# A graph network's third node stage: norm scale and shift moved into a copy, two bias matmuls removed, walk words loaded inside a batch

## Chip, core and metric

The kernel runs on one core of one Trainium2 chip. The metric is device time in microseconds (us), the median of several runs. The engines are PE (TensorE, matmuls; PEld is its loading of weights, PEldq or PEq its sequencer, which decodes instructions), DVE (VectorE), ACT (ScalarE), POOL (GpSimd) and SP (SyncE, here only a queue that issues DMAs). Each engine runs its own instructions in order; between engines there are only semaphores.

## The reference

Four graph layers over 50000 nodes of 128 floats, on 25000 edges, each followed by `x = layernorm(x + layer(x))`. The change touches how the third layer (GATv2, 4 heads) and the sums over neighbours of the layers before it are computed:

```
def _gatv2(x, ...):
    xl = (x @ Wl.T + bl).reshape(n, H, D)
    ...
    alpha = ex / (den[dst] + 1e-16)
    agg = segment_sum(xl[src] * alpha[:, :, None], dst, n)
    return agg.mean(axis=1) + conv_bias
h  = _gatv2(x, ...)
x1 = _layernorm(x + h, g1, beta1)             # (r - mean) * rstd * g1 + beta1
f  = gelu(x1 @ W1.T + b1) @ W2.T + b2
x  = _layernorm(x + _layernorm(x1 + f, g2, beta2))
```

The weights alpha of a node's edges sum to 1 in each head, so the mean over the heads of the bias bl comes out of a node's sum unchanged. All data is float32; a float32 matmul is two passes of the array in the trace, a bfloat16 one is one pass.

## The kernel before

The program is a chain of stages with a barrier after each. Three places matter.

**Walks** (`walk`, stages e0, e1a, e1b, before the second layer's node stage). POOL gathers the rows of the edges' sources (L998, 196 DMAs for each walk, four to a group). DVE makes one-hot matrices (L1013). PE adds six steps to a batch, 66 batches in a walk, 12 matmul instructions (24 passes, L1056) in each: `add_steps` first loads the batch's eight table words into registers with two loads of four (L1045), waits for the one-hots (L1049), the gathered rows (L1050) and begun tiles (L1051), and issues the matmuls, whose operands are addressed by these words. The body is a loop of three batches. ACT takes finished tiles out of PSUM.

**Edge sum** (`edge_sum` with `PrepareGatv2`, stage at 2123 to 2416 us). 196 chunks of 128 edges, in 28 groups of seven. For a chunk PE multiplies the source rows by Wl into one of seven PSUM banks (L1235, 512 columns) and adds the bias by a bfloat16 matmul with three rows (L1236). ACT scales the first head (L1221). DVE adds the other three (L1251), two chunks interleaved, and adds to each chunk the running sum of the chunk before it (L707); after a pair of chunks it waits for its last result and gives the banks back (L1264). After a group it waits again and signals (L713), and POOL scatters the group's seven chunks to DRAM by indirect DMAs (L684), only at rows where a node's edges end.

**Third node stage** (`node_gatv2`, names n_..., 2426 to 3207 us). 98 blocks of 512 rows, on a software pipeline: in every step of a loop of six each engine does its parts for blocks of different age, in an order written out at the end of its function (`pipeline(pe, (2, turn1), (7, product3), (6, turn3), (3, ffn2), (2, ffn1))`: the number is the age). For a block:
- DVE adds x and the edges' sum (L2247), takes statistics (L2254, L2263); POOL makes the reciprocal deviation and the shift (L1339 to L1345); ACT normalises (L1354).
- PE turns the rows over (L2329), ACT copies them out of PSUM (`move1`, L2373), PE multiplies by W1 (`ffn1`, L2336), ACT applies gelu (L2379).
- PE sums in one PSUM bank (`ffn2`): the biases by a bfloat16 matmul with three rows (L2301), x1 by a matmul with a diagonal of g1 (L2304), the product with W2 (L2307).
- DVE takes the second statistics from that bank (L2254, n_stats<-n_y_ps), POOL the deviation (L1332, L1334), DVE normalises (L2271), multiplies by g2 (L2277), adds the residual (L2282), takes third statistics; ACT normalises again (L1354, n_x3s), PE turns (L2315), ACT copies (L2361), PE multiplies by the next layer's weights (L2322), ACT keeps the result (L2367, L2368).

DVE's order in a step is: first add, second norm (four blocks back), first statistics, times g2, first aggregation, residual, second statistics (three back), third statistics, second aggregation, third aggregation. POOL's is: second deviation, third, first, then the addition of beta2. Before the loop DVE folds g1 into W1 and into the identity, and splits beta1 + b2 into three bfloat16 rows (L2233 to L2240); ACT spreads these by DMA.

## Time and profile before

| | us |
|---|---|
| median of 3 runs | 4979.55 (4978.65 to 4981.04) |
| the profiled execution | 4979.08 |
| its span in the trace | 4977.4 |
| busy PE / DVE / ACT / POOL | 3368.8 / 3292.8 / 2328.2 / 3358.2 |
| first, second, third walk, PE's first to last matmul | 137.7 to 382.9, 737.3 to 987.9, 998.1 to 1250.3 |
| edge sum, DVE's first to last chunk | 2128.4 to 2400.2 |
| third node stage | 2426 to 3207 |

Since stages end in barriers, the time is the sum of the stages, and each is read by itself: which engine waits for nothing there, or which closed chain of waits repeats. What the profile calls the chain that ended last covers only the final stage.

### The profile page before, as it was taken

What the parts mean: (1) busy time and instruction counts of PE and PEld (TensorE: products, weight loads), DVE (VectorE), ACT (ScalarE), POOL (GpSimd) and SP (SyncE); (2) the same over time, 40 slices, a digit from 0 to 9 for tenths busy, and PEclk for the clock granted to TensorE, in tenths of its full rate; (3) what the DMA queues carried; (4) which work ended last, traced back from release to release, by engine and by line L of the source; (5) the groups of instructions that cost most, each with busy time, mean ns of one, the idle gap of its engine ahead of it and who ended that gap; (6) DMA issues with size and microseconds to landing.
All of it is one profiled execution on the core that took longest, in us unless ns stands there. A gap on an engine that the chain in (4) does not pass through costs nothing. (4 is left out here: it accounts for less than half of the span.)

```text
span 4977.4 us, 95692 instructions
## 1 busy us (share of the span) xinstructions
PE 3368.8 (68%) x21145; PEld 2475.2 (50%) x21146; DVE 3292.8 (66%) x13393; ACT 2328.2 (47%) x6751; POOL 3358.2 (67%) x4041
## 2 busy tenths in 40 slices
PE   0778867777885999699599999730004999321666
PEld 0676757677563444322266666520003777221566
DVE  6987874454785777778588888650804888623676
ACT  0556767667674444333288888500002444000566
POOL 3746757677455777357588888676674555673998
PEclk9999989999998999899799999855557999655888
DMA  4447869888897412001144444352115988341676
GB/s 95 147 141 231 256 194 266 243 254 258 260 287 247 133 52 53 26 30 38 61 143 137 145 137 145 109 154 46 33 41 193 293 294 275 110 117 52 190 224 196
DMA packets 592362, 784.61 MB, mean 158 GB/s; under 512 B 138226, under 2 KB 362150, under 8 KB 591610
## 3 DMA queue, kind: packets, MB, share of 16 engines
q1 hardware_dynamic: 430496, 532.37, 35.0%
q0 software_dynamic: 62848, 112.43, 9.3%
q10 hardware_dynamic: 98846, 138.05, 7.6%
q14 instruction: 129, 1.06, 0.1%
q8 instruction: 43, 0.70, 0.1%
HBM read 470.23 MB, written 317.95 MB: 158 GB/s over the span
## 5 line engine op out<-in xcount | busy, mean ns | idle before, releaser
L2889 POOL TENSOR_SCALAR n_hot<-node_of,d_krel 128x256 f32<-128x256 f32 x396 | 381.1, 976 | 65.3 <-ACTq L2945 65.3
L1354 ACT ACTIVATE n_r<-n_r,n_shift,n_rstd 128x128 f32<-128x128 f32 x784 | 321.6, 480 | 67.7 <-POOL n_shift L1345 62.7
L2917 PE MATMUL n_bank<-h_rows,n_hot 128*128 x1584 | 241.8, 322 | 144.3 <-POOL n_hot L2889 144.1
L2917 PEld LDWEIGHTS n_bank<-h_rows,n_hot 128*128 128x128 f32 x1584 | 229.4, 232 | 157.4 <-issue 157.4
L684 POOL DMA_INDIRECT agg<-e_msg,e_put_i x196 | 194.8, 994 | 164.3 <-DVEq L713 113.0
L1354 ACT ACTIVATE n_o<-n_y_ps,n_shift,n_rstd 128x128 f32<-128x128 f32 x784 | 292.7, 454 | 13.5 <-POOL n_shift L1625 13.3
L968 POOL DMA_INDIRECT by_src<-by_src_pay,by_src_place_i x196 | 207.7, 1060 | 120.5 <-DVE n_o L1532 64.3
L998 POOL DMA_INDIRECT x_rows<-x,d_other_i x196 | 191.0, 974 | 119.2 <-POOLq L102 59.7
L615 POOL DMA_INDIRECT agg_dst<-e_rows,e_put_i x196 | 195.2, 996 | 102.2 <-issue 59.4
L2510 POOL TENSOR_TENSOR n_u<-n_u 128x512 f32<-128x512 f32 x98 | 124.6, 1271 | 205.7 <-DVE n_u L2457 205.7
L2639 POOL DMA_INDIRECT h_rows<-h,d_other_i x196 | 202.5, 1033 | 76.2 <-issue 59.4
L998 POOL DMA_INDIRECT y_rows<-y,s_other_i x196 | 186.2, 950 | 90.7 <-issue 53.4
L1341 POOL TENSOR_TENSOR n_rstd<-n_rstd,minus_half 128x4 f32<-128x4 f32 x196 | 235.2, 1200 | 15.4
L2011 POOL DMA_INDIRECT e_rows<-h,e_other_i x196 | 194.4, 992 | 73.8 <-issue 59.4
L1913 DVE TENSOR_TENSOR lg_z<-lg_z_ps,lg_z 128x512 f32<-128x512 f32 x196 | 135.3, 690 | 162.5 <-ACT lg_z L1879 162.5
L1056 PE MATMUL e1b_bank<-y_rows,e1b_hot 128*128 x1584 | 199.6, 285 | 60.4 <-ACT e1b_bank L1181 33.0
L2307 PE MATMUL n_y_ps<-n_w,n_gt 128*128 128x128 f32 x1568 | 240.5, 276 | 0.0
L1056 PE MATMUL e1a_bank<-y_rows,e1a_hot 128*128 x1584 | 198.7, 284 | 58.9 <-ACT e1a_bank L1167 30.1
L1834 POOL DMA_INDIRECT lg_rows<-x,e_other_i x196 | 186.0, 949 | 77.8 <-issue 59.4
L998 POOL DMA_INDIRECT y_rows<-m,s_other_i x196 | 186.1, 949 | 74.7 <-issue 57.3
L1235 PE MATMUL e_xl_ps<-gat_wl,e_xg 128*128 128x512 f32 x392 | 223.4, 652 | 18.0 <-ACT e_xg L1208 18.0
L1056 PE MATMUL e_bank<-x_rows,e_hot 128*128 x1584 | 197.1, 282 | 51.1 <-ACT e_bank L1139 42.2
(516 smaller groups left out, 11424.8 us busy)
## 6 DMA issues: line engine op xcount, KB each, us to landing
n_ag<-agg_dst SPq DMA_DIRECT2D x196, 264.0 KB
n_hs<-h SPq DMA_DIRECT2D x196, 264.0 KB
n_xs<-x SPq DMA_DIRECT2D x196, 256.0 KB, 4.3
agg_dst<-e_ev SPq DMA_DIRECT2D x196, 132.0 KB
y<-n_o ACTq DMA_DIRECT2D x98, 264.0 KB, 3.5
e1a_fed<-y SPq DMA_DIRECT2D x196, 132.0 KB
m<-e1a_ev SPq DMA_DIRECT2D x196, 132.0 KB
e1b_fed<-m SPq DMA_DIRECT2D x196, 132.0 KB
```

Of the source, the lines that this page charges most:

```text
L615: pool.indirect_dma_start(out=agg, out_offset=bass.IndirectOffsetOnAxis(ap=e.put_i[:, c:c + 1], axis=0), in_=rows[:, c, :], in_offset=None ...
L684: pool.indirect_dma_start(out=agg, out_offset=bass.IndirectOffsetOnAxis(ap=e.put_i[:, c:c + 1], axis=0), in_=msg[:, g % SLOTS, k, 0:out_wi ...
L968: return pool.indirect_dma_start(out=self.target, out_offset=bass.IndirectOffsetOnAxis(ap=self.place_i[:, c:c + 1], axis=0), in_=self.pay[ ...
L998: pool.indirect_dma_start(out=rows[:, c, 0:fetched], out_offset=None, in_=table, in_offset=bass.IndirectOffsetOnAxis(ap=e.other_i[:, c:c + ...
L1056: ins = pe.matmul(bank[:, bass.ds(to + h * width, summed)], hot[:, s, k, h * P:(h + 1) * P], flat_rows[:, bass.ds(row, summed)], start=Fal ...
L1235: pe.matmul(self.xl_ps[k][:, :], xg[:, s % 2, k, :], self.wl[:, :], start=True, stop=False)
L1341: st(pool.tensor_tensor(rstd, rstd, keep.minus_half[:, :], ALU.pow))
L1354: ins = act.activation(out[:, g, 0:D], r[:, g, :], ACT.Identity, bias=shift[:, g:g + 1], scale=rstd[:, g:g + 1])
L2307: ins = pe.matmul(y_ps[s % BANKS][:, g, :], gt[:, s % 2, j, g, :], w2[:, j, :], start=False, stop=(g, j) == (GB - 1, 1), skip_group_check= ...
L2639: pool.indirect_dma_start(out=rows[:, c, :], out_offset=None, in_=h, in_offset=bass.IndirectOffsetOnAxis(ap=on_dst.other_i[:, c:c + 1], ax ...
L2889: ins = pool.tensor_scalar(hot[:, i // STEPB % HOTS, i % STEPB, :], keep.node_of[:, :], e.krel[:, i:i + 1], None, ALU.is_equal)
L2917: ins = pe.matmul(bank[:, bass.ds(to + h * 256, SUMMED)], hot[:, s, k, h * P:(h + 1) * P], flat_rows[:, bass.ds(row, SUMMED)], start=False ...
```

## The change

- **Third node stage.** `move1` no longer copies: ACT's instruction computes scale times the turned rows plus shift, with g1 as scale and beta1 + b2 as shift, a number for each partition. `ffn2` loses its bias matmul, and adds x1 with the identity; W1 and the identity are used as they are. W1's product with b2 is taken from the first bias. DVE loses the preparation of the folded weights and of the three bfloat16 rows, ACT its three DMAs, SP two loads of weights (net). ACT waits until the weights are ready.
- **Edge sum.** PE's product has no bias matmul. One such matmul at the start spreads bl; DVE takes its mean over the heads. After each group DVE adds it to the seven finished chunks, 896 floats for each partition, into a buffer of its own (`whole`), which POOL scatters. The running sums are without it.
- **Walks.** Of the three batches in the loop's body, the first still loads its words at its start; those of the second and third are loaded within the batch before, four after the third step and four after the fifth.

```diff
@@ edge_sum
-        msg = ph.sb("msg", [P, SLOTS, GC, ROW])
+        msg, whole = ph.sb("msg", [P, SLOTS, GC, ROW]), ph.sb("whole", [P, SLOTS, GC, D])
...
-                                                in_=msg[:, g % SLOTS, k, 0:out_width], in_offset=None, bounds_check=bound,
+                                                in_=whole[:, g % SLOTS, k, 0:out_width], in_offset=None, bounds_check=bound,
...
                 dve.wait_ge(cleared, 1)
+                prepare.mean_bias(dve)
...
                         count.wait(count.n)
-                        dve.sem_inc(summed, 1)
+                        dve.tensor_tensor(whole[:, s], msg[:, s, :, 0:D], prepare.bias[:, :].unsqueeze(1).broadcast_to([P, GC, D]),
+                                          ALU.add).then_inc(summed, 1)
@@ walk
                         ins.then_inc(steps_done, 1)
+                        if s + 1 < HOTS and k in (2, 4):
+                            following += load_words(turn, s + 1, len(following))
+                    return following
 
                 with pe.Fori(0, BATCHES // HOTS) as turn:
+                    word = load_words(turn, 0, 0) + load_words(turn, 0, HALF_WORDS)
                     for s in range(HOTS):
-                        add_steps(turn, s)
+                        word = add_steps(turn, s, word)
@@ PrepareGatv2
-                pe.matmul(self.xl_ps[k][:, :], xg[:, s % 2, k, :], self.wl[:, :], start=True, stop=False)
-                pe.matmul(self.xl_ps[k][:, :], self.keep.ones_b[0:3, :], self.bl_parts[0:3, :],
-                          start=False, stop=True).then_inc(self.xl_ready, 1)
+                pe.matmul(self.xl_ps[k][:, :], xg[:, s % 2, k, :], self.wl[:, :], start=True, stop=True).then_inc(self.xl_ready, 1)
+
+            pe.matmul(self.xl_ps[0][:, :], self.keep.ones_b[0:3, :], self.bl_parts[0:3, :], start=True, stop=True)\
+                .then_inc(self.bias_spread, 1)
+            pe.wait_ge(self.bias_ready, 2)
...
+    def mean_bias(self, dve):
+
+        dve.wait_ge(self.bias_spread, 1)
+        dve.tensor_reduce(self.bias[:, :], self.xl_ps[0][:, :].rearrange("p (h d) -> p d h", h=HEADS), AX.X, ALU.add)\
+            .then_inc(self.bias_ready, 1)
+        dve.wait_ge(self.bias_ready, 1)
+        dve.tensor_scalar(self.bias[:, :], self.bias[:, :], 1.0 / HEADS, None, ALU.mult).then_inc(self.bias_ready, 1)
+        dve.wait_ge(self.bias_ready, 2)
@@ node_gatv2
-                link(dve.tensor_scalar(w1g[:, :, :], w1[:, :, :], column[:, 0:1], None, ALU.mult))
-                link(dve.tensor_scalar(g1_diag[:, :], keep.ident[:, :], column[:, 0:1], None, ALU.mult))
-
-                link(dve.tensor_tensor(vec["beta1"][:, :], vec["beta1"][:, :], vec["b2"][:, :], ALU.add))
-                split_bf16(dve, link, vec["beta1"][0:1, :], tmp[0:1, :], [p[:, :] for p in bias_part])
-                dve.sem_inc(parts_split, 1)
+                link(dve.tensor_tensor(joined[:, :], column[:, 1:2], column[:, 2:3], ALU.add))
                 dve.wait_ge(folded, 1)
-                link(dve.tensor_tensor(b1g[:, :], y_ps[0][:, 0, 0:2], b1[:, :], ALU.add))
+                link(dve.tensor_tensor(b1_less[:, :], b1[:, :], y_ps[0][:, 0, 0:2], ALU.subtract))
...
-                    pe.matmul(y_ps[s % BANKS][:, :, :], keep.ones_b[0:3, :], bias_parts[:, :, :], start=True, stop=False,
-                              skip_group_check=True)
                     for g in range(GB):
-                        pe.matmul(y_ps[s % BANKS][:, g, :], xt1[:, s, g, :], g1_diag[:, :], start=False, stop=False,
-                                  skip_group_check=True)
+                        pe.matmul(y_ps[s % BANKS][:, g, :], xt1[:, s, g, :], keep.ident[:, :], start=True, stop=False)
...
-                    act.activation(xt1[:, s], t1_ps[:, :, :], ACT.Copy).then_inc(moved1[s], 1)
+                    act.activation(xt1[:, s], t1_ps[:, :, :], ACT.Identity, bias=joined[:, 0:1], scale=column[:, 0:1]).then_inc(moved1[s], 1)
```

What stands on PE where one batch of a walk gives way to the next inside the loop (ISA: a register operation of the sequencer; REGISTER_ALU: a wait with a register; e1a_bank: the tiles' sums). Before:

```order
L1056 ISA
L1056 MATMUL e1a_bank<-y_rows,e1a_hot 128x128
L1045 ISA
L1045 TENSOR_LOAD s_table
L1045 ISA
L1045 TENSOR_LOAD s_table
L1049 REGISTER_ALU
L1050 REGISTER_ALU
L1051 REGISTER_ALU
L1056 ISA
L1056 MATMUL e1a_bank<-y_rows,e1a_hot 128x128
```

Now, from the second matmul of the fifth step on:

```order
L1060 MATMUL e1a_bank<-y_rows,e1a_hot 128x128
L1046 ISA
L1046 TENSOR_LOAD s_table
L1060 ISA
L1060 MATMUL e1a_bank<-y_rows,e1a_hot 128x128
L1060 ISA
L1060 MATMUL e1a_bank<-y_rows,e1a_hot 128x128
L1053 REGISTER_ALU
L1054 REGISTER_ALU
L1055 REGISTER_ALU
L1060 ISA
```

The same instructions stand there; the second load has moved up past one step, and the first past three.

DVE at the end of a group of the edge sum (e_cont: whether a chunk's row continues a node). Before:

```order
L1251 SCALAR_TENSOR_TENSOR e_msg<-e_xl_ps,alpha,e_msg 128x128 x3
L707 SCALAR_TENSOR_TENSOR e_msg<-e_msg,e_cont 128x128
L1251 SCALAR_TENSOR_TENSOR e_msg<-e_xl_ps,alpha,e_msg 128x128
L707 SCALAR_TENSOR_TENSOR e_msg<-e_msg,e_cont 128x128
L1251 SCALAR_TENSOR_TENSOR e_msg<-e_xl_ps,alpha,e_msg 128x128
L707 SCALAR_TENSOR_TENSOR e_msg<-e_msg,e_cont 128x128
L1251 SCALAR_TENSOR_TENSOR e_msg<-e_xl_ps,alpha,e_msg 128x128 x8
```

Now:

```order
L1271 SCALAR_TENSOR_TENSOR e_msg<-e_xl_ps,alpha,e_msg 128x128
L708 SCALAR_TENSOR_TENSOR e_msg<-e_msg,e_cont 128x128
L1271 SCALAR_TENSOR_TENSOR e_msg<-e_xl_ps,alpha,e_msg 128x128
L708 SCALAR_TENSOR_TENSOR e_msg<-e_msg,e_cont 128x128
L714 TENSOR_TENSOR e_whole<-e_msg,e_bias 128x896
L1271 SCALAR_TENSOR_TENSOR e_msg<-e_xl_ps,alpha,e_msg 128x128 x8
```

One instruction has come in between the last addition of a group and the first head of the next.

PE in a step of the third node stage (n_t_ps: turned rows; n_y_ps: the second norm's input). Before:

```order
L2315 MATMUL n_t_ps<-ident,n_x3s 128x128 x4
L2301 MATMUL n_y_ps<-n_bias_parts,ones_b 128x512
L2304 MATMUL n_y_ps<-n_g_diag,n_xt 128x128
L2307 MATMUL n_y_ps<-n_w,n_gt 128x128 x2
L2304 MATMUL n_y_ps<-n_g_diag,n_xt 128x128
```

Now:

```order
L2323 MATMUL n_t_ps<-ident,n_x3s 128x128 x4
L2313 MATMUL n_y_ps<-ident,n_xt 128x128
L2315 MATMUL n_y_ps<-n_w,n_gt 128x128 x2
L2313 MATMUL n_y_ps<-ident,n_xt 128x128
L2315 MATMUL n_y_ps<-n_w,n_gt 128x128 x2
```

The bfloat16 matmul is gone from between the turning and the first float32 product; all else keeps its place.

## Rows read from the trace of the kernel before

**Rows 1.** Busy times by stretch: us, PE, PEld, DVE, ACT, POOL, clock, DMA, GB/s

```profile
2120.00:2420.00 300.00, 272.86 (x590) 77.15 (x590) 225.34 (x789) 98.24 (x252) 196.86 (x198) 0.95 0.11 34
2420.00:3200.00 780.00, 701.50 (x4394) 516.52 (x4394) 632.85 (x3052) 596.09 (x1560) 627.50 (x1078) 0.97 0.40 134
```

**Rows 2.** Waits, third node stage: who <- whom, total us, times, longest

```profile
ACT n_x3s L1354 <- POOL n_shift L1345: 124.4, 95, 3.2
...
DVE n_stats L2254 <- PE n_y_ps L2307: 30.7, 49, 8.2
```

**Rows 3.** Timeline, third node stage: start, length, engine, instructions [idle before]

```profile
2800.98 1.37 DVE L2271 TENSOR_SCALAR n_r<-n_y_ps,n_mv,n_rstd 128x128 f32<-128x128 f32 x4 [1.00 <-POOL n_rstd L1334]
...
2806.52 0.20 POOL L1332 TENSOR_TENSOR n_rstd<-n_mv,eps 128x4 f32<-128x4 f32 x1 [0.39 <-DVE n_mv L2263]
...
2808.20 1.37 DVE L2271 TENSOR_SCALAR n_r<-n_y_ps,n_mv,n_rstd 128x128 f32<-128x128 f32 x4 [0.91 <-POOL n_rstd L1334]
...
2812.39 1.65 ACT L1354 ACTIVATE n_r<-n_r,n_shift,n_rstd 128x128 f32<-128x128 f32 x4 [0.25 <-POOL n_shift L1345]
...
2815.76 0.60 PE L2315 MATMUL n_t_ps<-ident,n_x3s 128*128 128x128 f32 x4
...
2816.94 0.61 PE L2307 MATMUL n_y_ps<-n_w,n_gt 128*128 128x128 f32 x4
...
2819.39 1.88 PE L2336 MATMUL n_f_ps<-n_xt,n_w1g 128*128 128x512 f32 x4
...
2819.59 0.89 DVE L2254 BATCH_NORM_STATS2 n_stats<-n_y_ps 128x6 f32<-128x128 f32 x4
...
2821.62 0.20 POOL L1332 TENSOR_TENSOR n_rstd<-n_mv,eps 128x4 f32<-128x4 f32 x1 [0.38 <-DVE n_mv L2263]
```

**Rows 4.** Groups of ACT, third node stage: names, shapes xcount | busy us, mean ns | idle

```profile
L2379 ACT ACTIVATE n_gt<-n_f_ps,n_b1g 128x512 f32<-128x512 f32 x194 | 123.1, 695 | 5.7 <-PE n_f_ps L2336 5.7
...
L2373 ACT ACTIVATE n_xt<-n_t_ps 128x512 f32<-128x512 f32 x98 | 60.3, 616 | 1.3 <-PE n_t_ps L2329 1.3
```

**Rows 5.** Timeline of VectorE where the third node stage starts

```profile
2438.59 0.35 DVE L2233 TENSOR_SCALAR n_w1g<-n_w,n_column 128x256 f32<-128x256 f32 x1
...
2441.11 0.16 DVE L2240 TENSOR_TENSOR n_b1g<-n_y_ps,n_b 128x2 f32<-128x2 f32 x1
```

**Rows 6.** Timeline of TensorE in the edge sum

```profile
2261.17 0.39 PE L1236 MATMUL e_xl_ps<-gat_bl_parts,ones_b 3*128 3x512 bf16 x1
...
2262.54 0.39 PE L1236 MATMUL e_xl_ps<-gat_bl_parts,ones_b 3*128 3x512 bf16 x1
```

**Rows 7.** Timeline of VectorE in the edge sum, where a group ends

```profile
2140.12 0.34 DVE L1251 SCALAR_TENSOR_TENSOR e_msg<-e_xl_ps,alpha,e_msg 128x128 f32<-128x128 f32 x1
2140.61 0.35 DVE L707 SCALAR_TENSOR_TENSOR e_msg<-e_msg,e_cont 128x128 f32<-128x128 f32 x1
2141.19 2.14 DVE L1251 SCALAR_TENSOR_TENSOR e_msg<-e_xl_ps,alpha,e_msg 128x128 f32<-128x128 f32 x7 [0.22 <-ACT e_msg L1221]
```

**Rows 8.** Lines of a later edge stage: op xcount: min/median/max ns, first and last start

```profile
L630 DVE TENSOR_TENSOR e_rows<-e_rows,e_weight x28: 1082/1092/1093, 3503.3 to 3609.5; 128x896 f32<-128x896 f32 x28
...
L615 POOL DMA_INDIRECT agg_dst<-e_rows,e_put_i x196: 982/982/1194, 3507.6 to 3761.2; - x196
```

**Rows 9.** Timeline of TensorE in the second walk, two batches

```profile
977.91 2.94 PE L1056 MATMUL e1a_bank<-y_rows,e1a_hot 128*128 x24 [0.83 <-POOLq L994]
981.55 2.94 PE L1056 MATMUL e1a_bank<-y_rows,e1a_hot 128*128 x24 [0.70 <-ACT e1a_bank L1167]
```

**Rows 10.** Lines of the walks (PEldq: TensorE's sequencer; first: 974.1 to 976.2 only)

```profile
L1056 PEldq FUSED_REGOPS  x11: 46/46/143, 974.2 to 975.9; - x11
...
L1045 PEldq TENSOR_LOAD <-d_table x132: 326/378/692, 133.4 to 379.4; - x132
...
L998 POOL DMA_INDIRECT y_rows<-y,s_other_i x196: 940/944/1083, 729.2 to 974.0; - x196
...
L998 POOL DMA_INDIRECT x_rows<-x,d_other_i x196: 940/944/1248, 73.3 to 322.8; - x196
```

More of the change, by code:

```diff
@@ L1039, in _, with load_words, add_steps @@
                 flat, flat_rows = e.table[:, :, :].rearrange("o b w -> o (b w)"), rows[:, :, :].rearrange("p j w -> p (j w)")
-                def add_steps(turn, s):
-                    why = "walk_tables counts steps, chunks and tiles"
-                    word = []
-                    for part in range(0, WORDS, HALF_WORDS):
-                        word += nc.values_load_multi_w_load_instructions(
-                            flat[0:1, bass.ds(turn * (HOTS * WORDS) + s * WORDS + part, HALF_WORDS)],
-                            engines=[mybir.EngineType.PE], min_val=0, max_val=(1 << 31) - 1,
-                            skip_runtime_bounds_check_because=why)[1]
+                why = "walk_tables counts steps, chunks and tiles"
+                def load_words(turn, s, part):
+                    return nc.values_load_multi_w_load_instructions(
+                        flat[0:1, bass.ds(turn * (HOTS * WORDS) + s * WORDS + part, HALF_WORDS)],
+                        engines=[mybir.EngineType.PE], min_val=0, max_val=(1 << 31) - 1,
+                        skip_runtime_bounds_check_because=why)[1]
+                def add_steps(turn, s, word):
+                    following = []
                     pe.wait_ge(hot_ready, turn * HOTS + s + 1)
@@ L1199, in start @@
         self.xl_ready, self.used, self.first_head = ph.sem("xl_ready"), ph.sem("used"), ph.sem("first_head")
+        self.bias, self.bias_spread, self.bias_ready = ph.sb("bias", [P, D]), ph.sem("bias_spread"), ph.sem("bias_ready")
         @block.scalar
@@ L2158, in node_gatv2 @@
         f_ps, h_ps = [ph.ps(f"f_ps{j}", [P, GB, P]) for j in range(2)], [ph.ps(f"h_ps{j}", [P, 2, ROW]) for j in range(2)]
-        bias_part, bias_parts = [ph.sb(f"bias_part{i}", [1, D], BF16) for i in range(3)], ph.sb("bias_parts", [3, GB, D], BF16)
-        parts_split, parts_in = ph.sem("parts_split"), ph.sem("parts_in")
         weights, chain, w_ready, folded = ph.sem("weights"), ph.sem("chain"), ph.sem("w_ready"), ph.sem("folded")
@@ L2180, in _ @@
                 sp.dma_start(wh[:, :], gat["W"]).then_inc(weights, 16)
-                for i, n in enumerate(("g1", "beta1")):
+                for i, n in enumerate(("g1", "beta1", "b2")):
                     sp.dma_start(column[:, i:i + 1], w[n].unsqueeze(1)).then_inc(weights, 16)
@@ L2291, in _ @@
                 for j in range(2):
-                    ins = pe.matmul(y_ps[0][:, 0, j:j + 1], w1[:, j, :], column[:, 1:2], start=True, stop=True)
+                    ins = pe.matmul(y_ps[0][:, 0, j:j + 1], w1[:, j, :], column[:, 2:3], start=True, stop=True)
                 ins.then_inc(folded, 1)
@@ L2298, in ffn2 @@
                     bank_free(pe, normed2, turn, s, 1, BANKS)
[L2299 to L2302 removed]
                     for g in range(GB):
[L2304 to L2305 removed]
+                        pe.matmul(y_ps[s % BANKS][:, g, :], xt1[:, s, g, :], keep.ident[:, :], start=True, stop=False)
                         for j in range(2):
                             ins = pe.matmul(y_ps[s % BANKS][:, g, :], gt[:, s % 2, j, g, :], w2[:, j, :], start=False,
[L2308 removed]
+                                            stop=j == 1)
                     ins.then_inc(y_ready[s], 1)
@@ L2335, in ffn1 @@
                     for j in range(2):
-                        ins = pe.matmul(f_ps[j][:, :, :], w1g[:, j, :], xt1[:, s], start=True, stop=True)
+                        ins = pe.matmul(f_ps[j][:, :, :], w1[:, j, :], xt1[:, s], start=True, stop=True)
                     ins.then_inc(f_ready[s], 1)
@@ L2343, in _ @@
                 ph.free_slots(act)
-                act.wait_ge(parts_split, 1)
-                for i in range(3):
-                    act.dma_start(bias_parts[i:i + 1, :, :], bias_part[i][:, :].unsqueeze(1).broadcast_to([1, GB, D])).then_inc(parts_in, 16)
+                act.wait_ge(w_ready, 1)
                 def first_norm(turn, s):
@@ L2378, in gelu @@
                     for j in range(2):
-                        act.activation(gt[:, s % 2, j], f_ps[j][:, :, :], ACT.Gelu, bias=b1g[:, j:j + 1]).then_inc(gelued[s], 1)
+                        act.activation(gt[:, s % 2, j], f_ps[j][:, :, :], ACT.Gelu, bias=b1_less[:, j:j + 1]).then_inc(gelued[s], 1)
                 pipeline(act, (3, gelu), (2, move1), (5, third_norm), (6, move3), (1, first_norm), (7, keep_h))
```

9 lines of the change are left out of this document (3 added, 6 removed).

## The prediction

> **What bounds the kernel now.** I read the table of stretches first: stages are separated by barriers, so each has its own bound and the busy shares of the whole span say nothing. In the third node stage PE is busy 701 of 780 us, in the edge sum 273 of 300 [rows 1]; both look bound by PE. The waits and the timeline then tell whether they are.
>
> *Third node stage.* In the timeline two closed chains show. The short one has DVE and POOL alone: DVE's second norm begins at 2800.98 and again at 2808.20, 7.22 us later. Between, DVE works through its order without waiting for PE, and POOL makes the next block's deviation from 2806.52 on [rows 3]. The long one spans two blocks. POOL starts at 2806.52; after its three deviations ACT's first norm starts at 2812.39; PE turns these rows in its next step and runs up to the second float32 sum; DVE's statistics of that sum start at 2819.59; POOL starts again at 2821.62. That is 15.10 us for two blocks, 7.55 each. So a block costs 7.5 us, and if PE never kept DVE waiting it would cost 7.2; the waits put 30.7 us in all on DVE waiting for that sum [rows 2]. PE is thus a link of a chain and not the bound.
>
> *Edge sum.* PE's cycle is 1.37 us for each chunk [rows 6], with no wait in it, 9.61 for a group of seven. Here PE is the bound, but DVE and POOL stand close behind.
>
> *Walks.* In the second walk a batch of matmuls starts each 3.64 us: 2.94 busy, 0.70 idle [rows 9]. POOL gathers from 729.2 to 974.0 [rows 10] and PE's matmuls run from 737.3 to 987.9, so the gathers pace this walk and its end is PE's. In the first walk the gathers end at 322.8 [rows 10], long before PE does (382.9), and PE sets the pace.
>
> **The change, part by part.** The profiled execution took 4979.1 us (span 4977.4 and 1.7 around it), 0.5 below the median of 4979.6; the sum is made against 4979.1.
>
> *PE in the node stage.* The bias matmul stands between four transposes, which start at 2815.76 and take 0.11 each, and the identity product, after which W2's starts at 2816.94 [rows 3]. Without it the products would follow at once: 2815.76 + 0.44 + 0.22 for the two passes = 2816.42. So 0.52 is won in each block; the bfloat16 matmul costs more than its columns because PE changes to it and back. The long chain passes this place once in two blocks: 15.10 - 0.52 = 14.58, or 7.29 a block. The short chain allows 7.22. A block therefore falls by 0.52 / 2 = 0.26, and 95 steady blocks by 25 us. Bounds: 10 us if other waits fill half of it, 31 us if all of DVE's wait for PE goes [rows 2]. What is late next is DVE and POOL's own chain, 0.07 behind.
>
> *ACT's copy.* It turns into scale and shift with two operands from SBUF. No row shows this form; on the same shape the gelu with one such operand took 0.695, the copy 0.616 [rows 4]. I take twice the difference, 0.16 more, with 0.08 and 0.24 as ends. It is hidden: ACT waits next for POOL's third shift, 124.4 us in 95 blocks, 1.3 each [rows 2], and PE needs the copy only at the end of its step. If that cover were gone it would cost up to 98 x 0.24 = 24 us. A gain is excluded, for it does more than the copy did.
>
> *Start of the node stage.* DVE's eight instructions from 2438.59 to 2441.11 [rows 5] give way to a single short one like that at 2441.11, 0.16: 2.4 us, and everything waits for them. SP issues two DMAs fewer ahead of the blocks' loads, which can only help; I take 3 us with them. ACT's new wait for the weights blocks nothing, since its first norm needs POOL, which waits for the same.
>
> *PE in the edge sum.* A chunk falls to two float32 passes. Four such passes of 512 columns span 1.88, the last counted 0.59 [rows 3], so 0.43 each: 0.86 a chunk, 6.0 a group.
>
> *DVE in the edge sum.* Its group without waits: 28 instructions, one each 0.26; where it waits for its own result 0.49 (2140.12 to 2140.61) and, at the group's end, 0.58 (2140.61 to 2141.19); seven in 2.14 with one such wait fit this [rows 7]. So 23 x 0.26 + 4 x 0.49 + 0.58 = 8.5 us. The added instruction has the very shape of one in a later stage, 1.09 [rows 8], of which 0.09 overlaps with the next: 9.5 us. This is the new bound, against 9.61 now: 0.1 x 27 groups = 3 us. The first group gains some 0.8, as PE's slow start shrinks, and the mean of the bias costs about as much at the start. I take 4; the ends are 0 (another 0.1 of wait in each group) and 14 (DVE hides it all and POOL decides, below).
>
> *POOL in the edge sum.* In the later stage with such DVE instructions beside it a scatter started each (3761.2 - 3507.6) / 195 = 1.30 us, 9.10 a group, and none took over 1.19 [rows 8]: POOL stays below DVE. The Trainium skill ("SBUF — State Buffer", the box on the "DVE blocks DMA" trap) speaks against the change: it says that GpSimd cannot write descriptors while a VectorE instruction holds the port that the two share. By that rule each group would cost POOL up to 1.09 more than 7 scatters, and the time would come out 20 us higher (D); the row shows far less.
>
> *Walks.* The idle 0.70 between batches looks like the price of the loads, but the sequencer's rows say otherwise. Its operand instructions, twelve to a batch, come at 974.2 to 975.9, eleven in 1.73 us, 0.173 apart; the array needs 2.94 for their 24 passes [rows 9, 10]. The sequencer runs ahead and is never held by the array: 12 x 0.173 = 2.1 for the steps, two loads with what stands around them, about 1, and 0.5 for three waits and the first matmul, which makes the 3.64. The sequencer is full, and moving its loads does not shorten it. I take 0. Bounds: the first walk's loads took 326 to 692 ns, half of them over 378 [rows 10]. If all took the shortest, it would gain some 132 x 0.1 = 13; if all took the longest, see C.
>
> **Sum.** 25 + 3 + 4 + 0 = 32: 4979.1 - 32 = 4947 us.
>
> **The rivals.**
>
> *A. PE was the bound after all.* Then each block gives the whole 0.52 (98 x 0.52 = 51 us), and the edge sum falls to POOL's 9.10 (0.51 x 27 = 14): 4979.1 - 51 - 3 - 14 = 4911. For it speaks PE's busy share; against it that a cycle of DVE and POOL, with no PE in it, already takes 7.22. 10%.
>
> *B. The words pay.* The gap of 0.70 goes in the 44 batches of the first walk whose words come early, 31 us; in the other walks, which the gathers pace, only in the last three batches, 2 us each: 4947 - 35 = 4912. For it speaks the visible gap, against it the sequencer's rows. 10%.
>
> *C. The loads get longer inside a batch: slower.* All 132 loads of each walk move to the long row, 0.69. First walk 132 x 0.3 = 40 us; in the other two the gathers give a slack of some 0.2 x 66 = 13, so 132 x 0.3 - 13 = 27 each. 4947 + 94 = 5041. It decides from where the mean load passes about 0.55, then the gain of 32 and another 10 are gone. For it: loads beside a busy DVE in the first walk are the longer ones; against it: they stood behind queued matmuls already, and half took 0.38 or less. 5%.
>
> *D. The port.* POOL's group is 9.10 + 1.09 = 10.2, the gain in the edge sum is lost, and 0.6 x 27 = 16 come on top: 4947 + 4 + 16 = 4967. Against it: the longest scatter beside such instructions was 1.19 [rows 8]. It would also follow from the skill's rule above. 5%.
>
> *E. Next to nothing.* The short chain in the node stage is longer than 7.22 in most blocks, as when POOL's part of it is stretched beside DVE, and the added instruction in the edge sum takes all of PE's gain: only the start and a few us remain, 4973. 8%.
>
> *PE's clock.* The granted clock was 0.95 and 0.97 of the 2.4 GHz level in the two stages [rows 1]. In the edge sum PE will be busy 6.0 of 9.5 us. At 1.2 GHz a group would need 12 us, but then PE would be busy without a gap, as it is now, when it is granted the higher level. I count it within the range.
>
> **How the numbers follow.** The forecast has 62%. The range must leave out no more than 20%: with A, B and D inside and C and E outside it leaves 13%, so it runs from 4905 to 4968. A measurement of this kernel tells 0.2%, 10 us, from no change. Faster by more: the forecast, A, B, D, and of the last a rest, 86%; within it E, 9%; slower C, 5%.
>
> **What would show it.** Right: steady blocks at 7.2 to 7.3 us, DVE's wait for the second sum near nothing, and its wait for POOL's deviation still there; groups of the edge sum at 9.5 with PE idle between chunks at a spacing of 0.86 within a pair, DVE without waits; POOL's scatters not over 1.2; walks of the same length, their gaps smaller and the steps spread out, with batches still at 3.6 us. Wrong: blocks below 7.1 (A), a first walk under 235 us (B), loads with a mean over 0.5 (C), a POOL scatter each 1.4 us (D), blocks above 7.4 (E).

## The result

The changed kernel takes 4934.94 us in the median of six runs (4928.56 to 4938.05), the kernel before 4979.10 (4977.34 to 4981.75): a ratio of 0.9912, with a 95% interval of 0.9903 to 0.9922. The forecast was 4947 with a range of 4905 to 4968. The profiled execution took 4934.43 us with a span of 4932.7.

### The profile after, beside that of before

I set marks at the same places in both traces and took the time between them: the first and last matmul of a walk, the edge sum's first instruction of VectorE (2123.9 before, 2115.8 after) and the end of its last scatter, POOL's first instruction of the third node stage and PE's last one.

| stretch | before | after | difference | forecast |
|---|---|---|---|---|
| up to the first walk | 137.7 | 136.0 | -1.7 | none |
| first walk | 245.5 | 241.1 | -4.4 | 0 |
| from there to the end of the third walk | 867.3 | 865.2 | -2.1 | 0 |
| from there to the edge sum | 873.4 | 873.5 | 0 | none |
| edge sum | 285.7 | 278.7 | -7.0 | -4 |
| start of the third node stage | 34.2 | 30.5 | -3.7 | -3 |
| its blocks | 761.8 | 737.3 | -24.5 | -25 |
| the rest | 1771.7 | 1770.4 | -1.3 | none |

The length of a step repeats to some hundredths from one trace to the next, that of a whole stage less well: the blocks of six kernels that have this node stage took 737.0 to 741.9 us, with filling and emptying of the pipeline.

The two stretches of [rows 1] in the trace after, moved to where the stages now lie (us, busy time of PE, PEld, DVE, ACT and POOL, granted clock, DMA share, GB/s):

```profile
2112.00:2412.00 300.00, 200.87 (x395) 74.42 (x395) 248.82 (x819) 98.15 (x252) 204.76 (x198) 0.89 0.11 34
2402.00:3182.00 780.00, 666.90 (x4332) 512.03 (x4332) 630.26 (x3046) 615.99 (x1569) 638.46 (x1090) 0.96 0.41 137
```

In the edge sum PE's busy time has fallen from 273 to 201 us and VectorE's has risen from 225 to 249. In the node stage PE, VectorE, ACT and POOL stand between 616 and 667 of 780 us.

The waits of the node stage after (who <- whom, us in total, times, longest), which answer to [rows 2]:

```profile
ACT n_x3s L1374 <- POOL n_shift L1365: 91.8, 98, 3.3
DVE n_r L2284 <- POOL n_rstd L1354: 81.9, 98, 1.2
...
POOL n_rstd L1352 <- DVE n_mv L2276: 46.2, 98, 5.9
...
DVE n_stats L2267 <- PE n_y_ps L2315: 13.2, 17, 8.7
```

VectorE's wait for the second float32 sum was 30.7 us with one of 8.2 in it; it is 13.2 with one of 8.7 in it (the pipeline's first block). Without that block it is 22.5 and 4.5. The wait for POOL's second deviation is still there in every block. The timeline of TensorE in one step (start, length), as in [rows 3]:

```profile
2706.24 0.60 PE L2323 MATMUL n_t_ps<-ident,n_x3s 128*128 128x128 f32 x4
2706.68 0.39 PE L2313 MATMUL n_y_ps<-ident,n_xt 128*128 128x128 f32 x2
2706.90 0.61 PE L2315 MATMUL n_y_ps<-n_w,n_gt 128*128 128x128 f32 x4
```

From the transposes to W2's first product there are now 0.66 us where there were 1.18 [rows 3]: the 0.52 of the forecast. The groups of ACT that answer to [rows 4] (busy us, mean ns):

```profile
L2385 ACT ACTIVATE n_gt<-n_f_ps,n_b_less 128x512 f32<-128x512 f32 x196 | 124.4, 696 | 5.4 <-PE n_f_ps L2344 5.4
L2379 ACT ACTIVATE n_xt<-n_t_ps,n_joined,n_column 128x512 f32<-128x512 f32 x98 | 78.2, 798 | 1.3 <-PE n_t_ps L2337 1.3
```

The copy with scale and shift takes 0.798 for 0.616 us. It is paid in ACT's wait for POOL: that is 91.8 us here and 109.1 in x4 below, which has the same blocks with the short copy.

The edge sum in VectorE's timeline, where one group ends and the next begins, answering to [rows 7]:

```profile
2205.13 0.35 DVE L708 SCALAR_TENSOR_TENSOR e_msg<-e_msg,e_cont 128x128 f32<-128x128 f32 x1
2205.51 1.09 DVE L714 TENSOR_TENSOR e_whole<-e_msg,e_bias 128x896 f32<-128x896 f32 x1
2206.53 2.39 DVE L1271 SCALAR_TENSOR_TENSOR e_msg<-e_xl_ps,alpha,e_msg 128x128 f32<-128x128 f32 x8
...
2214.85 1.09 DVE L714 TENSOR_TENSOR e_whole<-e_msg,e_bias 128x896 f32<-128x896 f32 x1
```

and POOL's scatters beside them:

```profile
2204.86 0.98 POOL L684 DMA_INDIRECT agg<-e_whole,e_put_i  x1 [0.30 <-issue]
2206.14 1.32 POOL L684 DMA_INDIRECT agg<-e_whole,e_put_i  x1 [0.30 <-issue]
2207.77 0.98 POOL L684 DMA_INDIRECT agg<-e_whole,e_put_i  x1 [0.31 <-issue]
```

A group takes 2214.85 - 2205.51 = 9.34 us, and 24 of 27 do to within 0.01. From 2130 to 2385 us VectorE waits for another engine only once, 0.5 us for ACT; its group is its own work and the waits for its own results. PE, with two passes a chunk, now waits 1.97 us in every group for VectorE to give banks back:

```profile
2203.56 2.84 PE L1244 MATMUL e_xl_ps<-gat_wl,e_xg 128*128 128x512 f32 x6 [0.33 <-DVEq L1284]
2208.36 1.96 PE L1244 MATMUL e_xl_ps<-gat_wl,e_xg 128*128 128x512 f32 x4 [1.97 <-DVEq L1284]
```

One scatter of seven lasts 1.32 us: it begins while VectorE's long instruction runs and ends 0.86 us after it. POOL has 9.34 - 7 x 1.287 = 0.33 us left in a group, and this is where it goes.

In the first walk, TensorE's matmuls and (after) its loads of words (ns: shortest, median, longest; first and last start), before and after:

```profile
L1056 PE MATMUL e_bank<-x_rows,e_hot x1584: 275/277/579, 137.7 to 382.9; 128*128 x198
```

```profile
L1060 PE MATMUL e_bank<-x_rows,e_hot x1584: 276/276/577, 136.0 to 376.8; 128*128 x198
...
L1046 PEldq TENSOR_LOAD <-d_table x132: 327/334/689, 131.7 to 372.9; - x132
```

The loads' median has fallen from 378 ns [rows 10] to 334, and their mean, taken over the single instructions, from 437 to 398. Only 88 of the 132 loads moved. The 44 behind the third step became shorter by 0.17 us in the mean (0.34 for 0.51), the 44 behind the fifth longer by 0.04 (0.42 for 0.38).

### The profile page after: what moved, and what is told of

It reads as the page before. It is cut to its first block and busy times, and to the rows that moved or that the text cites. A ratio compares the mean times of both kernels' runs of the same rounds, so it can differ in the third digit from the quotient of the medians.

```text
span 4932.7 us, 95098 instructions
## 1 busy us (share of the span) xinstructions
PE 3297.2 (67%) x20852; PEld 2470.8 (50%) x20853; DVE 3312.0 (67%) x13416; ACT 2347.0 (48%) x6751; POOL 3364.9 (68%) x4041
## 3 DMA queue, kind: packets, MB, share of 16 engines
q14 instruction: 129, 1.06, 0.1%
## 5 line engine op out<-in xcount | busy, mean ns | idle before, releaser
L684 POOL DMA_INDIRECT agg<-e_whole,e_put_i x196 | 202.7, 1034 | 149.5 <-DVE e_whole L714 90.1
L1060 PE MATMUL e1b_bank<-y_rows,e1b_hot 128*128 x1584 | 215.4, 288 | 43.6 <-ACT e1b_bank L1189 22.1
L1060 PE MATMUL e1a_bank<-y_rows,e1a_hot 128*128 x1584 | 214.9, 286 | 41.9 <-ACT e1a_bank L1175 15.9
L1244 PE MATMUL e_xl_ps<-gat_wl,e_xg 128*128 128x512 f32 x392 | 199.5, 648 | 59.8 <-DVEq L1284 58.7
L1060 PE MATMUL e_bank<-x_rows,e_hot 128*128 x1584 | 213.2, 287 | 30.4 <-ACT e_bank L1147 17.8
```

The source lines that it names most:

```text
L684: pool.indirect_dma_start(out=agg, out_offset=bass.IndirectOffsetOnAxis(ap=e.put_i[:, c:c + 1], axis=0), in_=whole[:, g % SLOTS, k, 0:out_ ...
L1060: ins = pe.matmul(bank[:, bass.ds(to + h * width, summed)], hot[:, s, k, h * P:(h + 1) * P], flat_rows[:, bass.ds(row, summed)], start=Fal ...
L1244: pe.matmul(self.xl_ps[k][:, :], xg[:, s % 2, k, :], self.wl[:, :], start=True, stop=True).then_inc(self.xl_ready, 1)
```

## The experiments

The runs of a kernel spread over up to 16 us on some chips (the kernel before from 4966 to 4982 in one set), more than some effects here. Each verdict below therefore rests on the stage's length in the trace, which repeats to within a few tenths for groups and blocks; the whole times stand beside it with their interval.

### One part of the change at a time

One line or two stand for each part; the rest is as in the diff of the change.

```diff
# x1: only node_gatv2 as changed
+                    act.activation(xt1[:, s], t1_ps[:, :, :], ACT.Identity, bias=joined[:, 0:1], scale=column[:, 0:1])
# x2: only edge_sum and PrepareGatv2 as changed
+                        dve.tensor_tensor(whole[:, s], msg[:, s, :, 0:D], prepare.bias[:, :]..., ALU.add)
# x3: only walk as changed
+                        if s + 1 < HOTS and k in (2, 4):
+                            following += load_words(turn, s + 1, len(following))
```

> The kernel before with the third node stage's part of the change alone. Theory (the prediction's, by its own steps): steady blocks at 7.28 us as in the changed kernel, the stage's start 2.4 to 3.7 us shorter, 28 us in all: about 4951. Rival 1, the parts help each other (the node stage's gain needs rows that the edge sum delivers earlier, or the like): less than 24 us of gain here. Rival 2, the stage's new gain is larger alone: over 32. The walks and the edge sum stay as before (edge sum 9.61 us a group).

Measured: 4945.45 us, ratio 0.9941 (0.9924 to 0.9957). The steady blocks take 7.28 us, the stage starts in 30.4 us as in the changed kernel, and walks and edge sum are as before (246.1 us for the first walk, groups of 9.61). From its first to its last second norm the stage takes 706.7 us (705.8 in the changed kernel, 729.4 before). With the start that is a gain of 26.5 us, and the whole times differ by 31 (21 to 38 by the interval). Taken from the edge sum's end to PE's last product, this one execution gives 23.7, a little under the 24 of rival 1: filling and emptying its pipeline took some 4 us longer than in the changed kernel, which x6, with the same stage, shows too (740.9 us for the blocks). So the gain of the steady blocks is the node stage's own, and rival 2 falls.

> The kernel before with the edge sum's part of the change alone. Theory: a group takes 9.34 us where it took 9.61, 27 times, 7 us in all: about 4972. Rival: some of the 7.4 us that the stage lost in the changed kernel came from elsewhere, and the group is at 9.5 or more. In the trace the seventh scatter of each group lasts 1.3 us, the other six 0.98.

Measured: 4970.72 us, ratio 0.9992 (0.9983 to 1.0002), which alone would show little. In the trace the groups take 9.34 us and the stage 277.8 us, 7.9 less than before; the blocks of the node stage take 7.53 as before.

> The kernel before with the walks' part of the change alone. The changed kernel's first walk was 4.4 us shorter, and the other two together some 2. Theory 1: this is the load instructions' own length (mean 0.438 us before, 0.398 after in the first walk), 132 x 0.04 = 5 us in the first walk, hence 4972 to 4975 and a mean load under 0.41 in the first walk again. Theory 2: nothing of the kind, the 6 us lie within what runs differ by; 4977 to 4981, and the mean load is as before, 0.43 to 0.45.

Measured: 4973.00 us, ratio 0.9994 (0.9985 to 1.0004). The first walk takes 242.2 us where the four kernels with the old walk took 244.8 to 246.1, and its loads 406 ns in the mean where these had 432 to 442. So theory 1 holds for the first walk, with 2.6 to 3.9 us for the 5 that it names; no trace with the new walk is over 242.2. From the end of the first walk to the end of the third this kernel took 867.9 us, and the four with the old walk 865.2 to 867.5: the 2.1 us that the changed kernel shows there are not the change's.

### The node stage: is PE the bound, and is ACT's copy hidden?

```diff
# x4: on the kernel before; the matmul with the diagonal of g1 starts the sum instead
-                    pe.matmul(y_ps[s % BANKS][:, :, :], keep.ones_b[0:3, :], bias_parts[:, :, :], start=True, stop=False,
-                              skip_group_check=True)
# x5: on the changed kernel; the product with W2 starts the sum instead
-                        pe.matmul(y_ps[s % BANKS][:, g, :], xt1[:, s, g, :], keep.ident[:, :], start=True, stop=False)
```

> The kernel before with nothing changed but that the third node stage's bias matmul is left out (beta1 + b2 are missing from the output's second norm): ACT still copies without scale and shift, the folded weights are still made. Theory: the whole gain of the steady blocks is the bias matmul's, and ACT's longer copy (0.80 for 0.62 us) is hidden: blocks at 7.28 us, about 4979 - 24 = 4955. Rival: the longer copy costs something, and the blocks here are at 7.2 or less: 4947 or less.

Measured: 4953.10 us, ratio 0.9952 (0.9936 to 0.9968), blocks of 7.28 us. With ACT's short copy they are as long as with the long one (7.28 in the changed kernel, to the hundredth in nearly every step). The bias matmul is the whole of the blocks' gain, and the copy is hidden.

> The changed kernel without the product with the identity in the third node stage (x1 is missing from the second norm's input): 8 passes of PE fewer in each block, 0.9 us of its work. Theory: PE is a link of a chain and no longer the later one; DVE and POOL's own chain holds, and the blocks fall from 7.28 to 7.21 us at most, 7 us in all. Rival, PE was the bound all along: each block gives the whole 0.9, 6.4 us, 86 us in all.

Measured: 4938.36 us, ratio 0.9931 (0.9914 to 0.9947): no faster than the changed kernel. The rival falls by far. For some 30 blocks the theory held: a turn of six took 6.95 + 7.30 + 4 x 7.21 = 43.1 us, 7.18 a block, for 7.28. After that one block in each turn of six took 8.12 us, and in more than half of the turns another took about 7.5 for 6.95; the mean came to 7.39. Windows of that trace (us, busy PE, PEld, DVE, ACT, POOL, granted clock):

```profile
2600.00:2650.00 50.00, 39.78 (x248) 29.04 (x247) 43.88 (x218) 43.38 (x112) 44.68 (x77) 1.00 0.42 147
2650.00:2700.00 50.00, 41.96 (x246) 31.89 (x246) 43.16 (x209) 42.66 (x109) 43.30 (x75) 0.93 0.42 140
2738.00:2741.00 3.00, 3.00 (x17) 3.00 (x18) 2.49 (x9) 2.32 (x5) 2.69 (x7) 0.58 0.44 158
2741.00:2744.00 3.00, 3.00 (x16) 2.31 (x16) 2.18 (x12) 2.74 (x8) 2.73 (x4) 0.85 0.14 35
```

The changed kernel, where the same stretch was granted the full clock:

```profile
2650.00:2700.00 50.00, 45.46 (x300) 34.73 (x300) 43.60 (x214) 43.46 (x112) 44.20 (x75) 1.00 0.44 149
```

PE had become less busy (39.8 of 50 us for 45.5), and once or twice in a turn it was then granted 1.2 GHz for some 3 us: 0.58 of the 2.4 GHz level in the window from 2738 to 2741, 0.85 in the next. In just that step VectorE waits for PE's sum again:

```profile
2738.51 1.37 DVE L2284 TENSOR_SCALAR n_r<-n_y_ps,n_mv,n_rstd 128x128 f32<-128x128 f32 x4 [0.91 <-POOL n_rstd L1354]
...
2742.93 0.89 DVE L2267 BATCH_NORM_STATS2 n_stats<-n_y_ps 128x6 f32<-128x128 f32 x4 [0.82 <-PE n_y_ps L2314]
...
2746.63 1.37 DVE L2284 TENSOR_SCALAR n_r<-n_y_ps,n_mv,n_rstd 128x128 f32<-128x128 f32 x4 [0.91 <-POOL n_rstd L1354]
```

The step is 8.12 us long, the usual 7.21 and this wait of 0.82 nearly all of the rest. What PE did less was given back by its clock. That the lower clock came of the lighter load is what the two traces suggest, since nothing else differs between them in this stage. How it came of it is not shown, and the busy share alone does not decide it. In the edge sum, where PE has less to do without its bias matmul, the clock was 0.96 in the changed kernel, but 1.00 in x11 (below) with PE no busier. The first row is the changed kernel's, the second x11's:

```profile
2150.00:2360.00 210.00, 157.39 (x314) 57.26 (x312) 195.44 (x652) 78.89 (x203) 162.48 (x157) 0.96 0.12 39
2150.00:2360.00 210.00, 154.87 (x320) 54.87 (x319) 198.76 (x687) 80.19 (x206) 161.09 (x161) 1.00 0.12 40
```

### The edge sum: VectorE or POOL?

```diff
# x6: on the changed kernel
-                        dve.tensor_tensor(whole[:, s], msg[:, s, :, 0:D], ..., ALU.add).then_inc(summed, 1)
+                        dve.sem_inc(summed, 1)
-                                                in_=whole[:, g % SLOTS, k, 0:out_width], ...
+                                                in_=msg[:, g % SLOTS, k, 0:out_width], ...
# x7: on the changed kernel; early() is called ahead of the wait that ends the last chunk's heads
+                        prepare(dve, turn, s, msg, count, add_before, lambda: finish(0, 4))
                         count.wait(count.n)
-                        dve.tensor_tensor(whole[:, s], msg[:, s, :, 0:D], ..., ALU.add).then_inc(summed, 1)
+                        finish(4, GC - 4).then_inc(summed, 1)
```

> The changed kernel without VectorE's addition to the finished group in the edge sum; POOL scatters the running sums themselves (the bias is missing from the rows). Theory: VectorE sets the pace of 9.34 us a group; without its 1.02 it could do 8.3, and POOL is then the bound at seven scatters of 1.287, 9.0 to 9.1 us, 6 to 9 us less in the stage; the long seventh scatter (1.31 us) is gone. Rival: POOL sets the 9.34 already by that long scatter; then the group falls to the same 9.0 but in this run the first scatter of a group starts later and later after VectorE's signal, where in the changed kernel it starts 1.16 us after it in every group. Second rival: ACT or PE holds at 9.3, nothing changes.

Measured: 4927.96 us, ratio 0.9904 (0.9888 to 0.9921). A group takes 9.0 to 9.17 us, (2387.0 - 2134.9) / 195 x 7 = 9.05 in the mean, and no scatter is over 1.15:

```profile
L684 POOL DMA_INDIRECT agg<-e_msg,e_put_i x196: 982/982/1146, 2134.9 to 2387.0; - x196
```

Here POOL is the bound, and it can be told from the lag: the first scatter of a group starts 0.9 us after VectorE's last addition of it in the first group and 13.8 us after it in the last, 0.48 more each time. VectorE alone needs 9.05 - 0.48 = 8.57 us in the mean (8.53 in most groups), more than the 8.3 that was expected. In the changed kernel the same lag is 2.29 us in all 27 later groups, and VectorE waits for no other engine in them but once (0.5 us): there POOL keeps up and VectorE sets the pace. How VectorE's group ends here explains the 8.53:

```profile
2206.15 0.37 ACT L1229 ACTIVATE e_msg<-e_xl_ps,e_alpha_s 128x128 f32<-128x128 f32 x1 [1.38 <-PE e_xl_ps L1243]
...
2211.04 0.35 DVE L708 SCALAR_TENSOR_TENSOR e_msg<-e_msg,e_cont 128x128 f32<-128x128 f32 x1
...
2211.61 0.61 DVE L1270 SCALAR_TENSOR_TENSOR e_msg<-e_xl_ps,alpha,e_msg 128x128 f32<-128x128 f32 x2 [0.22 <-DVE e_msg L708]
```

From the last addition to the next group's first head there are 0.57 us, as in the kernel before [rows 7], though ACT had been ready with that head for 5 us. They are VectorE's wait for its own result and its signal. With L714 in between, L714 follows the last addition after 0.38 and the next head follows L714 after 1.02, 1.40 in all: the instruction costs 0.83 and not its whole 1.02. Why the wait is shorter where the signal rides on an instruction is not shown.

> The changed kernel with that addition in two instructions: the first four chunks ahead of the last pair's wait, the last three at the end. VectorE's work is 0.08 more and two of its waits (0.23 and 0.12) are filled: 0.15 to 0.25 less a group. Theory, VectorE is the bound: 9.1 to 9.2 us, 4 to 6 us less in the stage. Rival, POOL is: an instruction of VectorE's holds up the scatter beside it, the two hold up one or two scatters, and the group stays at 9.3 or goes above.

Measured: 4930.21 us, ratio 0.9911 (0.9895 to 0.9928). Groups of 9.17 us, as the theory had it, and 255.1 us from first to last scatter where the changed kernel took 261.1:

```profile
L687 POOL DMA_INDIRECT agg<-e_whole,e_put_i x196: 981/982/1073, 2129.8 to 2384.9; - x196
```

VectorE again waits for another engine only once (0.5 us), and POOL is there when the group is signalled. A scatter that begins within the first of the two shorter instructions (0.68 and 0.56 us) is held up by 0.08, where the changed kernel's was held up by 0.33; another 0.08 goes where a scatter begins within an addition of the running sum. In each of these cases the held scatter ends 0.86 us after the instruction that it began in.

### The walks: is the sequencer full?

```diff
# x8: on the changed kernel
                         if s + 1 < HOTS and k in (2, 4):
+                            load_words(turn, s + 1, len(following))
                             following += load_words(turn, s + 1, len(following))
# x9: the same, with the second copy used
+                            twice += load_words(turn, s + 1, len(twice))
-                        row = ... word[k] % (1 << ROW_BITS) ...
+                        row = ... again[k] % (1 << ROW_BITS) ...
```

> The changed kernel with each load of words inside a batch issued twice, the first result unused: 88 loads more in each walk. Theory, TensorE's sequencer is full and waits for nothing: each costs its 0.33 to 0.45 us and 0.16 around it, 0.5 in all; the first walk is 44 us longer, the other two, which the gathers pace with little slack, 35 us each; about 5050. Rival, loads inside a batch are hidden behind queued matmuls: the walks keep their length and the time is 4935.

Measured: 4936.79 us, which says nothing: the trace has 132 loads in a walk as before. The copies, which nothing read, are not in it. The kernel is the changed one once more (first walk 241.6 us, blocks 7.28), and x9 was made so that both copies are read.

> The changed kernel with each load of words inside a batch issued twice, and both results used (rows and one wait read the second, targets the first), so that 88 loads more stand in the trace of each walk. Theory, TensorE's sequencer is full and waits for nothing: each costs its 0.33 to 0.40 us and 0.06 after it, 0.39 to 0.46; the first walk is 34 to 40 us longer (275 to 281), the other two, which the gathers pace with some 0.1 us of slack a batch, 28 to 34 us each; 5025 to 5045. Rival, loads inside a batch are hidden behind queued matmuls: the walks keep their length and the time is 4935.

Measured: 5036.19 us, ratio 1.0120 (1.0103 to 1.0137). The first walk takes 278.1 us, the other two 280.2 and 280.0:

```profile
L1060 PE MATMUL e_bank<-x_rows,e_hot x1584: 275/277/579, 137.0 to 414.8; 128*128 x198
...
L1046 PEldq TENSOR_LOAD <-d_table x220: 327/333/667, 132.7 to 410.9; - x110
```

Against the 241 to 242 us of the other kernels with loads inside the batch, 36 to 37 us for 88 loads are 0.42 each: a load (0.39 in the mean here) and what stands around it. In this walk the sequencer hides nothing of them behind the array, even inside a batch.

### Two edits that the traces pointed to

In the changed kernel POOL waits for VectorE only 0.3 us in a steady block, and VectorE works through the third statistics (0.8 us) before the aggregation that POOL waits for.

```diff
# x10: on the changed kernel; x11: with x7's edit besides
                 pipeline(dve, ..., (3, statistics(1, y_ready, ...)),
-                         (4, statistics(2, residual, ...)), (3, together(1, sums2)), (4, together(2, sums3)))
+                         (3, together(1, sums2)), (4, statistics(2, residual, ...)), (4, together(2, sums3)))
# x12: x11 with
-                        if s + 1 < HOTS and k in (2, 4):
+                        if s + 1 < HOTS and k in (0, 2):
```

> The changed kernel with one instruction of VectorE's order moved in the third node stage: the second norm's aggregation right behind its statistics, ahead of the third statistics (0.8 us earlier). POOL, which waits for it 0.32 us a block, then starts as soon as it is free. Theory, the blocks are set by the closed chain of VectorE and POOL: they fall by up to those 0.32, to 6.95 to 7.1 us, 18 to 32 us in all: 4903 to 4917. Rival, VectorE's own wait for the statistics it has just issued (0.2 us) and the third aggregation, which now comes alone, take it back: 7.25 to 7.4.

Measured: 4916.24 us, ratio 0.9875 (0.9858 to 0.9891). Blocks of 7.05 us in the mean, most of them 6.8 and 7.3 in turn. The waits of its node stage:

```profile
DVE n_mv L2276 <- DVE n_stats L2267: 28.9, 187, 0.2
DVE n_stats L2267 <- PE n_y_ps L2315: 28.5, 39, 8.6
...
POOL n_rstd L1352 <- DVE n_mv L2276: 23.6, 38, 5.9
```

POOL's wait has halved, and VectorE hardly waits for POOL any more (1.4 us, twice, where it was 81.9); it waits for its own statistics (0.15, twice a block) and again for PE, in 39 blocks. So the blocks had been set by the closed chain of VectorE and POOL, as the prediction read it. Now VectorE's own order sets most steps, and the chain through PE the others.

> The addition in the edge sum in two instructions and the earlier aggregation together. The two stages have a barrier between them, so their gains should add: 6 us of the first and whatever the second gives: 4897 to 4911 by its theory, 4929 or more by its rival.

Measured: 4909.61 us, ratio 0.9867 (0.9851 to 0.9883). Groups of 9.17, blocks of 7.06: the gains add. It is 22 to 25 us below the changed kernel (by the ratios and by the medians), and no kernel of the study is faster by more than the measurement tells.

> The two edits of the run before (addition in two instructions, earlier aggregation), and in the walks the loads inside a batch stand behind the first and the third step instead of the third and the fifth. In the first walk the loads behind the third step took 0.33 to 0.36 us in the mean, those behind the fifth 0.40 to 0.43. Theory 1, what stands ahead on the sequencer within the batch sets it (few matmuls issued since the batch's waits make a load short): the early places take 0.33 to 0.36 both, the walk falls by 44 x 0.07 = 3 us to 238. Theory 2, the place behind the third step is the lucky one, by what VectorE and ACT do at that moment, and not the earliness: the load behind the first step takes 0.40 or more and the walk stays at 241 or is longer. The whole kernel: 4905 to 4911 in both.

Measured: 4910.26 us, ratio 0.9865 (0.9849 to 0.9882). The early loads took 333 to 363 ns in the mean for each of the four places (332 to 430 in the changed kernel). So theory 2 falls, and theory 1 is right on the loads, though not on the walk: it stayed at 241.0 us, as in x11, where 238 was expected. Why a load behind more matmuls is longer is not shown. Of the 0.036 us that a batch's loads gave, its first wait, for the one-hot matrices, took 0.028. So the sequencer begins to wait for VectorE.

## Why the prediction was right, point by point

*Which chain bounds the node stage, and the 0.52.* Right. The bias matmul was worth 0.52 on PE and 0.25 a block, as a chain of two blocks that passes it once would have it (forecast 0.26; 23.6 us between the first and the last norm). That the whole stage gives 24.5 for 25 is closer than the lengths of that stage repeat. x4 shows that no other edit had a part in it, and x5's first turns that PE had hardly more to give (7.18 for 7.28). That the price of 0.52 comes of the change of type, as the prediction says, is not shown: the matmul also differs in having three rows.

*ACT's copy.* Taken at 0.16 more, it is 0.18 more, and hidden (x4 against the changed kernel).

*Start of the stage.* 3.7 for 3 us.

*Edge sum.* The mechanism was right: PE's work fell below VectorE's, which became the bound with POOL close behind. The step that was mis-sized is VectorE's group, 9.5 where 9.34 was measured, and with it the term: 4 for 7 us. The group without the new instruction was taken rightly at 8.5 (8.53 in x6). The instruction was then added with 1.0, and it costs 0.81 (9.34 less 8.53): it stands where VectorE waited for its own result, and that stretch has shrunk from 0.57 to 0.38. The 0.22 before the next head, which [rows 7] put down to ACT, stand in x6 with ACT ready long before; they are not a wait for ACT that went away. The forecast also had POOL's scatters at no more than 1.2; one in seven is at 1.32. The later stage of [rows 8], which spoke against rival D, had the same instruction of 1.09 us, but its scatters began elsewhere beside it:

```profile
3506.82 1.09 DVE L630 TENSOR_TENSOR e_rows<-e_rows,e_weight 128x896 f32<-128x896 f32 x1
3507.60 1.19 POOL L615 DMA_INDIRECT agg_dst<-e_rows,e_put_i  x1 [42.78 <-DVEq L642]
...
3510.77 1.09 DVE L630 TENSOR_TENSOR e_rows<-e_rows,e_weight 128x896 f32<-128x896 f32 x1
3511.78 0.98 POOL L615 DMA_INDIRECT agg_dst<-e_rows,e_put_i  x1 [0.30 <-issue]
```

The one that began 0.31 us before the instruction's end took 1.19; the other 26 began 0.08 before it and took 0.98. In the edge sum 23 of 27 began 0.45 to 0.47 before it and took 1.31 to 1.33, the longest began 0.72 before and took 1.58. So the row could not price D, and that D cost nothing is in part luck: rival D, the port, named the right thing at the wrong price. The scatter is held to the end of VectorE's instruction, but that took 0.33 of a group and not 1.09, and POOL had it to spare. The Trainium skill ("SBUF — State Buffer", the box on the "DVE blocks DMA" trap) says that GpSimd is kept from writing descriptors while VectorE runs an instruction in a mode that takes the shared port pair. The trace bears out the direction for this addition of two operands from SBUF, and a scatter loses no more than what of the instruction is left when it begins.

*Walks.* Taken at 0, the first walk gave 4.4 us in the changed kernel and 2.6 to 3.9 in x3. That the sequencer is full and that the gap is no gap to be closed was right (x9: 0.42 us for each further load). What failed is that moving the loads shortens nothing. The load's length had been put between its bounds (13 us of gain if all took the shortest) and the value taken was no change. Inside the batch the 44 loads behind the third step are shorter by 0.17 us, the 44 behind the fifth longer by 0.04; over all 132 that is 0.04 shorter in the mean. Rival B (235 us or less) and rival C (longer loads) both fall.

*The clock.* I had counted it within the range. In the edge sum's stretch it was 0.89 for 0.95, and from 2150 to 2360 us, within the groups, 0.96 for 1.00. It cost nothing that the groups show, since PE has 1.97 us of waiting in each. In the node stage it was 0.96 for 0.97.

*The rest.* The profiled executions differ by 44.7 us where 32 was forecast. Of the 12.7 between, 3 are the edge sum's, 4.4 the first walk's, 0.7 the stage's start, less 0.5 for the blocks, and 5.1 lie in stretches that the change does not touch, or does not shorten as x3 shows for the later walks. Single executions differ by as much there: from the node stage's end to the end of the program, which is the same in both, x2 took 1765.0 us and the kernel before 1771.7.

## What to carry to other kernels

When an engine looks busiest, look for a closed chain without it: the time from one start to the next of an instruction whose waits never reach that engine is the floor that relieving it can bring, and a relief on a chain of two blocks is worth half of its price. A chain's next step is then to issue first what the other engine waits for; here that was worth some 20 us for one moved line, nearly as much as the bias matmul. A load more in the sequencer's full stream cost its whole length, inside a batch too. A row that shows no harm says little unless the two instructions overlap in it as they will in the new place.

## What the runs showed of the hardware

- With PE relieved its granted clock fell, which cost more than the relief gave: with 39.8 us of work in 50 for 45.5 it was granted 1.2 GHz for some 3 us once or twice in each turn of six blocks, and one block in six went from 7.21 to 8.12 us (x5). That the lighter load brought it on is suggested by the two traces, not shown apart.
- A scatter of 0.98 us that begins while VectorE adds two operands from SBUF ends 0.86 us after that instruction or later: it takes 1.32 us with 0.46 of the instruction left, 1.58 with 0.72, 1.06 with 0.20 (x7), and still 0.98 with 0.08. One that began with the instruction (0.02 us after its start, x7) was not held. In the changed kernel, where the instruction comes once in a group, the two are in step: the scatter loses 0.33 us, just what POOL has to spare.
- A load of four words into TensorE's registers took 0.33 to 0.36 us in the mean behind two or six matmuls of a batch, 0.41 to 0.43 behind ten (first walk, changed kernel and x12), and single ones up to 0.69. What it waits for stays open.
